# The replicated stores of the leftover block pair: dealt to ScalarE and GpSimd, and spread between tiles

## The reference, cut to what matters

```
h = relu(layernorm(x))                 # x: 2708 x 512
h = relu(adj @ (h @ W1) + b1)          # adj: 2708 x 2708, dense in the kernel; W1: 512 x 1024
h = relu(adj @ (h @ W2) + b2)          # W2: 1024 x 1024
h = adj @ (h @ W3) + b3                # W3: 1024 x 512
out = x + h
```

## Time and profile before

| | |
|---|---|
| median of 3 runs (lowest, highest) | 1592.54 us (1591.84, 1593.34) |
| the profiled execution | 1593.69 us, of which the span of the trace is 1591.5 us |
| PE busy | 1571.2 us, 99% of the span |
| PE weight loads busy | 1352.5 us, 85% |
| DVE busy | 878.5 us, 55% |
| ACT busy | 644.2 us, 40% |
| POOL busy | 527.6 us, 33% |
| granted PE clock, mean | 0.997 of full speed |
| DMA | 336.34 MB, mean 211 GB/s |

### The profile page before, as it was taken

One profiled execution on the slowest core, in us unless ns is written; L12 is line 12 of the kernel. 1 busy time (PEld: TensorE's weight loads), 2 busy tenths in 40 slices (PEclk: granted clock), 3 DMA queues, 4 the chain that ended last, 5 costly groups with the idle time before them and its releaser, 6 DMA issues.

```text
span 1591.5 us, 21100 instructions
## 1 busy us (share of the span) xinstructions
PE 1571.2 (99%) x7622; PEld 1352.5 (85%) x7622; DVE 878.5 (55%) x1366; ACT 644.2 (40%) x1145; POOL 527.6 (33%) x492
## 2 busy tenths in 40 slices
PE   9999999999899999999999999999999999999999
PEld 7888889988688888889898989888898878888899
DVE  8983433255353456443545344774665536676766
ACT  5442222234243423333323333533455536555555
POOL 4863544336365544100000003573302334031312
PEclk9999999999999999999999999999999999999999
DMA  6956657554587888554557567783645358898887
GB/s 241 343 187 230 218 180 216 178 162 151 172 260 248 295 268 299 166 167 129 170 179 216 160 201 246 261 272 109 188 121 132 84 149 265 254 319 269 255 268 229
DMA packets 210655, 336.34 MB, mean 211 GB/s; under 512 B 22740, under 2 KB 95820, under 8 KB 210552
## 3 DMA queue, kind: packets, MB, share of 16 engines
q1 hardware_dynamic: 169900, 239.24, 49.0%
q0 software_dynamic: 16128, 56.88, 10.8%
q10 hardware_dynamic: 24524, 38.89, 7.1%
HBM read 244.78 MB, written 90.14 MB: 210 GB/s over the span
## 4 chain that ended last, share of the span: by engine, by line
PE 89%; DVE 7%; DMA 2%; ACTq 1%; ACT 1%; issue 1%; DVEq 0%
PE ps L1885 29%; PE ps L1886 28%; PE ps L1887 28%; DVE slots L1469 2%; PE ps L1979 2%; PE ps L1978 2%; DVE still L1451 1%; DVE stats L1399 1%; DVE ring L1490 0%; DMA raw<-HX 0%; DMA H<-spill 0%; DMA raw<-TS 0%; ACTq L925 0%; PE ps L1923 0%; DVE spread L1415 0%
## 5 line engine op out<-in xcount | busy, mean ns | idle before, releaser
L1490 DVE TENSOR_TENSOR ring<-raw,ring 128x512 fp32r<-128x512 f32 (+1 forms) x522 | 375.9, 735 | 412.4 <-ACT ring L1236 410.3
L1236 ACT CAST ring<-raw 128x512 fp32r<-128x512 f32 (+1 forms) x564 | 319.7, 576 | 493.7 <-PE ps L1887 370.9
L1885 PE MATMUL ps<-slots,still 128*128 128x512 f32 (+1 forms) x504 | 184.3, 366 | 2.9 <-DVE still L1435 1.5
L1887 PE MATMUL ps<-slots,still 128*128 128x512 f32 (+1 forms) x504 | 184.0, 365 | 0.0
L1886 PE MATMUL ps<-slots,still 128*128 128x512 f32 (+1 forms) x504 | 184.0, 365 | 0.0
L1885 PE MATMUL ps<-ring,even 128*128 128x512 f32 (+1 forms) x480 | 174.3, 363 | 0.0
L1886 PE MATMUL ps<-ring,even 128*128 128x512 f32 (+1 forms) x480 | 174.3, 363 | 0.0
L1887 PE MATMUL ps<-ring,even 128*128 128x512 f32 (+1 forms) x480 | 174.3, 363 | 0.0
L1885 PE MATMUL ps<-ring,S 128*128 128x512 f32 (+1 forms) x420 | 153.1, 365 | 0.9 <-DVE ring L1490 0.9
L1886 PE MATMUL ps<-ring,S 128*128 128x512 f32 (+1 forms) x420 | 152.8, 364 | 0.0
L1887 PE MATMUL ps<-ring,S 128*128 128x512 f32 (+1 forms) x420 | 152.8, 364 | 0.0
(11 more groups left out here) (176 smaller groups left out, 3020.6 us busy)
## 6 DMA issues: line engine op xcount, KB each, us to landing
raw<-TS SPq DMA_DIRECT2D x160, 256.0 KB, 3.4
raw<-adjT SPq DMA_DIRECT2D x122, 256.0 KB, 3.8
raw<-adjT SPq DMA_DIRECT2D x41, 512.0 KB, 4.8
TS<-made SPq DMA_DIRECT2D x20, 1024.0 KB, 6.7
raw<-TS SPq DMA_DIRECT2D x80, 165.0 KB, 2.9
raw<-HS SPq DMA_DIRECT2D x50, 256.0 KB, 3.1
raw<-P SPq DMA_DIRECT2D x45, 256.0 KB, 3.9
raw<-H SPq DMA_DIRECT2D x42, 256.0 KB, 3.1
```

The source lines that it names most:

```text
L1236: act.copy(hi, src).then_inc(hi_done, 1)
L1490: dve.tensor_tensor(lo, src, hi.bitcast(F32), ALU.subtract).then_inc(lo_done, 1)
L1885: pe.matmul(out, st_hi, mv_hi, start=start, stop=False)
L1887: return pe.matmul(out, st_lo, mv_hi, start=False, stop=stop)
```

## The change

`KEPT` is now the count of one set, 9 DMAs of 16. `store_full` and `store_short` each store one set, and `store_full` is further cut into thirds of two DMAs. A new kind of step, "lay", stands for one such lot. The planner puts, behind block 20, the three lots of set 1 at once, and the three lots of set 0 behind 0, 1 and 2 further cuts; behind block 21 one lot of each set. ACT does the lots of set 0, POOL those of set 1, each waiting for the relu or the copy. Each phase and set has a semaphore of its own (`set_stored`), where there was `kept_stored` of the pair's buffer in h1 and `kept3_stored` in w3. POOL waits for both sets before it reads back; SP waits only for the set that it reads (X11 is in set 0, X12 in set 1). In the first group of pass3 the load of the extra stack stands behind the sixth moving cut in place of the third.

```diff
-KEPT = 18
+KEPT = 9 * 16
@@ plan_main
+    def lay(phase, b, buf, number):
+
+        for third in range(1 if b == SHORT else 3):
+            p.later(third, lambda third=third: p.steps.append(("lay", (phase, b, buf, 0, third, number))))
+            p.steps.append(("lay", (phase, b, buf, 1, third, number)))
@@ h1_phase
                 if pair_of(b) == EXTRA:
+                    lay("h1", b, (turn, side), p.relu)
                     if side == 1:
@@ w3_phase
                 if pair_of(b) == EXTRA:
-                    p.steps.append(("keep", (b, buf, p.copied)))
+                    lay("w3", b, buf, p.copied)
@@ pass3
-                    if i == 2:
+                    if i == (2 if ends else 5):
@@ gcn_kernel
-        def store_full(engine, where, tile, stored):
-
-            for k in range(2):
-                rows = tile[k * MOST:(k + 1) * MOST]
-                first, second = where(k, 0), where(k, 1)
+        def store_full(engine, phase, k, third, tile):
+
+            first, second = (set_rows(phase, k, stack) for stack in range(2))
+            stored = set_stored[phase, k]
+            rows = tile[k * MOST:(k + 1) * MOST]
+            if third == 0:
                 engine.dma_start(first[0:MOST], rows).then_inc(stored, 16)
                 engine.dma_start(first[REST:REST + STEP], rows[0:STEP]).then_inc(stored, 16)
+            elif third == 1:
                 engine.dma_start(first[REST + STEP:P], rows[STEP:AGAIN]).then_inc(stored, 16)
                 engine.dma_start(second[0:MOST], rows).then_inc(stored, 16)
+            else:
                 for row in (MOST, LOW):
                     engine.dma_start(second[row:row + MOST + STEP - REST], rows[REST - STEP:MOST]).then_inc(stored, 16)
+        def lay(engine, phase, b, buf, k, third, number):
+
+            if phase == "h1":
+                turn, side = buf
+                tile = pair_buf[:, turn % PAIR_BUFS, side, :]
+                engine.wait_ge(relu_done, number)
+            else:
+                tile = buffer(buf)
+                engine.wait_ge(copied, number)
+            tile = tile.rearrange("p (s f) -> p s f", s=2)
+            if b == SHORT:
+                store_short(engine, phase, k, tile)
+            else:
+                store_full(engine, phase, k, third, tile)
@@ sync
                 elif j.kind == "extra2":
-                    if "extra" not in seen:
-                        seen["extra"] = 1
-                        i = extra_turn % PAIR_BUFS
-                        sp.wait_ge(kept_stored[i], kept(i, extra_turn + 1))
+                    if j.part in (X11, X12) and j.half == 0:
+                        sp.wait_ge(set_stored["h1", j.part], KEPT)
@@ scalar
-                    stored = kept_stored[turn % PAIR_BUFS]
-                    if g.block == 20:
-                        act.wait_ge(relu_done, n)
-                        store_full(act, kept1, tile.rearrange("p (s f) -> p s f", s=2), stored)
-                    elif g.block == SHORT:
-                        act.wait_ge(relu_done, n)
-                        store_short(act, kept1, tile.rearrange("p (s f) -> p s f", s=2), stored)
-                    elif side == 1:
+                    if side == 1 and pair_of(g.block) != EXTRA:
@@
-                elif kind == "keep":
-                    b, buf, n = a
-                    tile = buffer(buf).rearrange("p (s f) -> p s f", s=2)
-                    act.wait_ge(copied, n)
-                    (store_short if b == SHORT else store_full)(act, kept3, tile, kept3_stored)
+                elif kind == "lay" and a[3] == 0:
+                    lay(act, *a)
@@ gpsimd, combine1
-                pool.wait_ge(kept_stored[i], kept(i, turn + 1))
-                if pair == EXTRA:
+                if pair != EXTRA:
+                    pool.wait_ge(kept_stored[i], kept(i, turn + 1))
+                else:
+                    for k in range(2):
+                        pool.wait_ge(set_stored["h1", k], KEPT)
@@ gpsimd, the loops over the steps (the same for "w3")
             for kind, a in steps:
+                if kind == "lay" and a[0] == "h1" and a[3] == 1:
+                    lay(pool, *a)
                 if kind == "combine" and a[0] == "h1":
                     combine1(*a[1:])
```

More of the change, by code:

```diff
@@ L814, in gcn_kernel @@
         combined = sem("combined")
-        kept3_stored = sem("kept3_stored")
+        set_stored = {(s, k): sem(f"{s}_set_stored{k}") for s in ("h1", "w3") for k in range(2)}
         extra_in = sem("extra_in")
@@ L901, in kept @@
             mine = [t for t in range(turns) if t % PAIR_BUFS == i]
-            return 16 * (len(mine) + (KEPT - 1) * (extra_turn in mine))
+            return 16 * (len(mine) - (extra_turn in mine))
         def sums(i):
@@ L935, in kept1, with store_short @@
-        def kept1(k, stack):
-            return HX[2 * k:2 * k + 2, stack].rearrange("s p f -> p s f")
-        def kept3(k, stack):
-            return HX3[2 * k:2 * k + 2, :, stack * QUARTER:(stack + 1) * QUARTER].rearrange("s p f -> p s f")
+        def store_short(engine, phase, k, tile):
+            stored = set_stored[phase, k]
+            rows = tile[k * TAIL // 2:(k + 1) * TAIL // 2]
+            engine.dma_start(set_rows(phase, k, 0)[MOST:REST], rows).then_inc(stored, 16)
+            for row in (LOW, P):
+                engine.dma_start(set_rows(phase, k, 1)[row + MOST - REST:row], rows).then_inc(stored, 16)
@@ new lines, in set_rows @@
+        def set_rows(phase, k, stack):
+            if phase == "h1":
+                return HX[2 * k:2 * k + 2, stack].rearrange("s p f -> p s f")
+            return HX3[2 * k:2 * k + 2, :, stack * QUARTER:(stack + 1) * QUARTER].rearrange("s p f -> p s f")
+        def lay(engine, phase, b, buf, k, third, number):
+            if phase == "h1":
+                turn, side = buf
[9 more added lines that the diff above has]
+                store_full(engine, phase, k, third, tile)
@@ L1026, in _ @@
             seen = {"p1": 0, "h2": -1}
-            waited = []
             def wait_h1():
@@ L1098, in load @@
                 elif j.kind == "extra3":
[L1099 to L1102, removed]
+                    if j.part in (X11, X12):
+                        sp.wait_ge(set_stored["w3", j.part], KEPT)
+                    elif j.part != X22 and "sums3" not in seen:
+                        seen["sums3"] = 1
+                        sp.wait_ge(sums3_stored, 128)
                     sp.dma_start(raw[:, r, :], HX3[EXTRA_PLACE[j.part], :, :]).then_inc(raw_in[r], 16)
@@ L1339, in _ @@
                         act.wait_ge(stat_lo, w3_early)
-                        act.wait_ge(kept3_stored, 16 * KEPT)
+                        for k in range(2):
+                            act.wait_ge(set_stored["w3", k], KEPT)
                         act.wait_ge(sums3_stored, 128)
@@ L1674, in combine1 @@
                 a1, a2, z1, z2 = A[:, 0:F], A[:, F:H], B[:, 0:F], B[:, F:H]
-                pool.wait_ge(kept_stored[i], kept(i, turn + 1))
-                if pair == EXTRA:
+                if pair != EXTRA:
+                    pool.wait_ge(kept_stored[i], kept(i, turn + 1))
+                else:
+                    for k in range(2):
+                        pool.wait_ge(set_stored["h1", k], KEPT)
                     for k, tile in enumerate((A, B)):
-                        pool.dma_start(tile.rearrange("p (s f) -> p s f", s=2), kept1(k, 0)).then_inc(extra_in, 16)
+                        pool.dma_start(tile.rearrange("p (s f) -> p s f", s=2), set_rows("h1", k, 0)).then_inc(extra_in, 16)
                     pool.wait_ge(extra_in, 32)
@@ L1708, in combine3 @@
                 if pair == EXTRA:
-                    pool.wait_ge(kept3_stored, 16 * KEPT)
+                    for k in range(2):
+                        pool.wait_ge(set_stored["w3", k], KEPT)
                     for k, tile in enumerate((A, B)):
-                        pool.dma_start(tile.rearrange("p (s f) -> p s f", s=2), kept3(k, 0)).then_inc(extra_in, 16)
+                        pool.dma_start(tile.rearrange("p (s f) -> p s f", s=2), set_rows("w3", k, 0)).then_inc(extra_in, 16)
                     pool.wait_ge(extra_in, 64)
@@ L1854, in _ @@
             for kind, a in steps:
+                if kind == "lay" and a[0] == "w3" and a[3] == 1:
+                    lay(pool, *a)
                 if kind == "combine" and a[0] == "w3":
```

## The result

| | before | after |
|---|---|---|
| median of 5 runs, us (lowest, highest) | 1593.11 (1591.84, 1595.12) | 1584.63 (1581.77, 1586.22) |
| profiled execution, us | 1593.69 | 1582.82 |
| span of its trace, us | 1591.5 | 1580.6 |
| PE busy, us | 1571.2 | 1569.5 |
| ACT, POOL busy, us | 644.2, 527.6 | 643.5, 537.9 |

The ratio is 0.9943, with a 95% interval of 0.9928 to 0.9957: 8.5 us faster at the median, where I had forecast 14.8. The time lies above the range that I gave (1575.0 to 1582.6).

A forecast was written before the change was run, and what follows sets the result against it. PE bounds the kernel (busy 1571.2 of 1591.5 us), so only its idle time and lowered clock can be won. 11.7 + 3.8 - 0.4 - 0.3 = 14.8 us off 1592.5 gave 1577.7, stated as 1577.8; range 1575.0 to 1582.6.

The forecast's parts named there:

- The full prize: PE's pauses and low clock in h1 (11.7 us) and w3 (3.8 us), together 15.5 us to be won.
- Part 1, the first pause: In h1, block 18's cut comes in time behind lot 0 (1.3 us), so PE's 6.1 us pause goes entirely.
- Part 1, block 9's cut: In h1, lot 1 at 1.5 us and block 21's lot at 1.1 ahead of it leave a PE pause of 0.4 us.
- part 4: POOL gains nine issues per phase, some 5.5 us; in h1 they end at about 425 us and delay nothing.
- rival A: In h1 the lots are dear to issue, so the pause shrinks but stays: 1580.1 to 1581.8 us; chance 0.14.
- My own sign: In h1, the forecast is wrong if ACT's lot 1 costs over 2 us.
- my worst end: In h1, lot 1 at 1.72 + 2.04 us, giving a PE pause of 2.7 us ahead of block 9.
- Part 2: At the start of pass2, PE waits 0.3 us for the third cut; 0 to 4.6 us possible.
- rival B: DVE beside POOL's sums bounds the start of pass2; third cut 3 us late, 4.6 with low clock: 1582.1 us; chance 0.10.
- Part 3: In w3, both PE waits and ACT's 5.58 us of issue idle go: 3.8 us gained.
- rival C: In w3, POOL's issues at 4.1 us each beside DVE's stationaries hold up pass3: slower, 1604.5 us; chance 0.03.
- Rival D: The gain is given back later, DMA or another engine holding pass2 to old times: 1589 to 1593 us; chance 0.03.

The follow-up runs named there:

- spread_only: The changed kernel with ACT issuing all 18 stores of a phase, in lots spread behind 0 to 5 further cuts, GpSimd none: 1575.34 us, ratio 0.9892.
- undone_hs_held: As h1_undone, but GpSimd's two stores of pair 7's sums wait until block 18's cut is made: 1585.65 us, ratio 0.9959.
- again: The changed kernel run once more with no edit: 1582.52 us, ratio 0.9938 against the kernel before.
- pool_waits: The changed kernel, but in h1 GpSimd's lots wait until block 9's cut has been made: 1577.86 us, ratio 0.9908.
- deal_only: The changed kernel without the spreading: ACT issues set 0 at once and GpSimd set 1 at once, in both phases: 1584.05 us, ratio 0.9948.
- sp_deals: The changed kernel, but set 1 of h1 is issued by SyncE in place of GpSimd: 1578.31 us, ratio 0.9904.
- h1_undone: The changed kernel with h1's stores as before, ACT issuing all 12 and 6 at once behind the two relus: 1588.00 us, ratio 0.9976.

## Why the prediction was wrong, point by point

- **The full prize was right.** I had 11.7 us for h1. In six profiles, of five kernels, the stretch from relu to pass2 is 24.46 us to 0.01, whatever else differs between them: 36.17 - 24.46 = 11.7. With w3's 3.8 that makes 15.5; spread_only gained 17.4 at the median, with an interval of 14.3 to 20.1.
- **Part 1, the first pause:** right. Lot 0 was 1.3 us, block 18's cut was ready in time.
- **Part 1, block 9's cut: the step that failed.** Ahead of it I priced lot 1 at 1.5 us and block 21's lot at 1.1; they measured 1.9 and 5.4 us in the first profile. This is the term of the sum that was mis-sized. Two readings are behind it. I took the dear issues of rows 5 for the effect of a run of twelve, which undone_hs_held refutes: without GpSimd's two stores the same run is cheap. And I gave block 21's lot a single price, from a time in which POOL issued nothing (rows 4, at 433 us), and no upper bound, although I had written in part 4 that POOL would issue until about 425, and in rival A that its six stores would be under way. The condition that I should have named is that GpSimd issues nothing meanwhile. My own sign, lot 1 at over 2 us, did not show it in the first profile either (1.85; in *again* 2.4), as it was set on the wrong lot.
- **The choice between the ends.** The pause of 0.4 us was 3.5 to 3.9. Even my worst end, 2.7, was short, though it had 3.8 us for lot 1, which took 1.9 to 2.4: it had no upper bound for block 21's lot. Two terms erred the other way and hid some of it. In the first profile the relu of block 21 began 0.6 us ahead of my count, from block 20's relu on, and lot 1 began with it (420.51) and not 1.1 us later, behind its end.
- **The low clock** was priced in rival A alone, at 1.7 us; the main sum had none. It cost some 1.4 us.
- **Rival A was the right mechanism**, at too low a price (1580.1 to 1581.8 against 1582.8 in the profiled execution, and 1584.6 and 1582.5 as medians) and too low a chance. Beside it I cited the Trainium skill, "DMA: Bandwidth & Descriptors", section "Issuing engines are not separate DMA queues". The trace agrees with its first half, that the DMAs of all issuers share the engines, as far as ACT's five issues take 7.3 us beside POOL's burst and 2.9 without. Its second, that the issue time is small relative to the DMA, does not help here: 12 issues held up ACT for 11.96 us (rows 4), and that is where the gain lay.
- **Part 2 and rival B:** no pause of over 0.9 us at the first cuts of pass2 in any kernel, and none in the changed one but for 0.2 us. DVE made two of them in 3.47 us in the profile after, as in rows 6, with enough ahead.
- **Part 3, w3:** right, 23.11 - 19.26 = 3.85 us for 3.8. The issues there stayed at 0.35 to 0.62 us on ACT. I can't say why they stayed cheap: the stores are half the width, but the engines were full there too, with a DMA share of 0.95 to 1.08 over five of the nine issues (lines 932, 933, the two of 936, and 942).
- **Part 4 and rival C:** POOL's issues in w3 cost 0.55 to 0.64 us beside DVE's stationaries, and its idle time ahead of pair 8's sums was 4.0 us for 4.79. The port rule of the Trainium skill, "SBUF — State Buffer", which I set beside C, is not seen in any of these rows; its 3.1 us are for a DVE copy, and the stationaries are TENSOR_TENSOR.
- **Rival D:** no. What h1 gave in the second row of the table is still there at pass3's start (1315.47 - 1303.96 = 11.5 us, the sum of three rows), and only 0.6 us of it went in pass3.

## What to carry to other kernels

A DMA issue is a piece of work on the engine that issues it, and whatever stands behind it in that engine's order waits; move it behind the work that is due first, a few at a time. Its price is not a constant: when a change makes a second queue issue at the same moment, take the price from rows in which other queues issued as much. Spreading transfers in time and dealing them to another queue look like two halves of one idea. Here each gained by itself (17.4 and 8.7 us), but the second took back 7 to 8 us of the first, so they are to be timed apart.

## What I had not expected of the hardware

- ACT's issue of the same DMA costs 0.29 us or 2.50 us (block 21's first), and lot 2's two 0.7 or 4.3 us, by what other queues issue beside it or just ahead of it. The dear ones came at a DMA share of 0.8 to 1.0 over their own time, but that share alone doesn't tell. Block 21's last two took 1.13 us in pool_waits at a share of 0.95 (423.36 to 424.49), and in *again* the first of them alone 3.08 at the same share. In deal_only its first took 0.28 us at a share of 1.01. What the share lacks is not shown here.
- SyncE's issues stretch in the same way (0.33 to 1.82 us in sp_deals), GpSimd's don't: 0.54 to 0.75 us in every profile between 400 and 465 us, at a DMA share of 1.0 as at less. So a burst from GpSimd is not slowed at its issue, and ACT's issues beside it are (7.3 us for 2.9).
- ACT's sequencer issues a DMA while its own activation still runs (they start at 420.50 and 420.51 us in the changed kernel), as long as the DMA waits for something older.
- The pause of 2.5 us in w3 (rows 8) was not followed by a lowered clock: 1.00 is granted from 1294 to 1300 us. Those of 3.5 to 3.9 us in h1 were, with 3.4 us at the lower level in the first profile after and in deal_only and 6.8 in *again*. The second pause of h1, 1.83 us, was followed by 3.4 us of it in the kernel before, that of 1.74 us in h1_undone by none.
